# Splitting work on GpSimd and half of a broadcast copied on chip by ScalarE, in a recommendation tower (one core)

## The reference, cut to what matters

```python
e = jnp.stack([tbl_f[ids[:, f]] for f in range(39)], axis=1)      # (2048, 39, 16)
xk = x0 = e
for idx, (W, b) in enumerate([(w0, b0), (w1, b1), (w2, b2)]):     # W: (39, fk, 128), fk = 39, 64, 64
    z = relu(einsum('bhd,bkd,hks->bsd', x0, xk, W) + b[None, :, None])
    if idx != 2:
        xk = z[:, :64, :]; direct.append(z[:, 64:, :])
    else:
        direct.append(z)
logit = sum(concatenate(direct, axis=1), axis=-1)                 # (2048, 256)
h = relu(concat([logit, dense_ctx]) @ W_top1 + b_top1)
h = relu(h @ W_top2 + b_top2);  y = h @ W_top3
```

## Time and profile before

| | us |
|---|---|
| median of 3 runs | 2626.81 (2619.22 to 2628.51) |
| the profiled execution, its own time | 2621.27 |
| its span | 2619.4 |
| PE busy | 2487.5 (95%) |
| DVE busy | 2452.1 (94%) |
| POOL busy | 973.6 (37%) |
| ACT busy | 866.4 (33%) |
| mean share of 16 DMA engines | 0.8 to 0.9 in most of the span |

### The profile page before, as it was taken

How to read it: one execution, slowest core, us unless ns; L and a number is a source line. 1 busy time by engine, 2 the same in 40 slices (tenths; PEclk the granted TensorE clock), 3 DMA queues, 4 the chain that set the end, 5 groups by cost and what they waited for, 6 DMA issues and landing times.

```text
span 2619.4 us, 28223 instructions
## 1 busy us (share of the span) xinstructions
PE 2487.5 (95%) x7350; PEld 1370.7 (52%) x7350; DVE 2452.1 (94%) x2375; ACT 866.4 (33%) x853; POOL 973.6 (37%) x674
## 2 busy tenths in 40 slices
PE   0699999999999999999999999999999999999978
PEld 0355555555555555555555555555555555555546
DVE  2599999999999999999999999999999999999982
ACT  0133333233333323333332333333233333333325
POOL 7570542608163360726336071633607262000000
PEclk9899999999999999999999999999999999999999
DMA  3997888998888898888888988888898788888710
GB/s 82 224 213 176 193 176 194 193 201 193 182 189 179 191 194 196 197 181 192 179 192 188 205 195 181 187 178 190 188 204 214 163 188 177 191 181 195 176 46 8
DMA packets 184305, 469.76 MB, mean 179 GB/s; under 512 B 37746, under 2 KB 74211, under 8 KB 184275
## 3 DMA queue, kind: packets, MB, share of 16 engines
q1 hardware_dynamic: 160941, 461.79, 78.2%
q0 software_dynamic: 19968, 5.15, 2.1%
q10 hardware_dynamic: 3367, 2.48, 0.4%
HBM read 456.96 MB, written 12.33 MB: 179 GB/s over the span
## 4 chain that ended last, share of the span: by engine, by line
PE 38%; DVE 28%; DMA 15%; issue 13%; ACT 2%; SPq 1%; DVEq 1%; POOL 0%; ACTq 0%
PE zacc_a L811 17%; PE zacc_b L811 15%; DMA spread<-x_periods 14%; DVE prod L705 13%; DVE low L676 7%; DVE prod L693 5%; PE zacc_a L846 2%; PE zacc_b L846 2%; DVE high L676 1%; ACT maps L549 1%; DMA shifted<-x_periods 1%; ACT high L578 1%; ACT maps L548 1%; SPq L422 1%; DVE half L712 1%
## 5 line engine op out<-in xcount | busy, mean ns | idle before, releaser
L705 DVE TENSOR_TENSOR prod<-spread,maps 128x1024 f32<-128x1024 f32 (+1 forms) x1280 | 1493.8, 1208 | 27.8 <-DMA spread<-x_periods 18.0
L578 ACT ACTIVATE high<-prod 128x1024 fp32r<-128x1024 f32 (+2 forms) x544 | 575.0, 1057 | 1452.8 <-DVE prod L705 1207.0
L483 POOL DMA_INDIRECT landed<-in_tbl,rows_id x624 | 953.3, 1528 | 237.5 <-issue 235.5
L811 PE MATMUL zacc_a<-prod,w_plain 128*128 128x512 f32 (+2 forms) x1920 | 881.9, 595 | 19.7 <-DVE prod L693 15.0
L811 PE MATMUL zacc_b<-prod,w_plain 128*128 128x512 f32 (+2 forms) x1920 | 877.9, 593 | 5.3 <-DVE prod L705 5.3
L676 DVE TENSOR_TENSOR low<-prod,high 128x1024 fp32r<-128x1024 f32 (+1 forms) x480 | 581.7, 1212 | 0.0
L811 PEld LDWEIGHTS zacc_a<-prod,w_plain 128*128 128x128 f32 (+2 forms) x1920 | 363.8, 190 | 362.3 <-issue 328.1
L811 PEld LDWEIGHTS zacc_b<-prod,w_plain 128*128 128x128 f32 (+2 forms) x1920 | 363.9, 190 | 347.3 <-issue 308.4
L489 POOL TENSOR_TENSOR mark<-mark 128x1 f32<-128x1 f32 x30 | 16.6, 553 | 973.2 <-PE maps L858 967.6
L693 DVE TENSOR_TENSOR prod<-shifted,x_thrice 117x1024 f32<-117x1024 f32 (+1 forms) x224 | 264.8, 1214 | 50.8 <-DMA shifted<-x_periods 49.3
L846 PE MATMUL zacc_a<-low,w_high 128*128 128x512 f32 (+1 forms) x480 | 234.8, 570 | 12.2 <-DVE low L676 12.2
(11 more groups left out here) (101 smaller groups left out, 821.7 us busy)
## 6 DMA issues: line engine op xcount, KB each, us to landing
spread<-x_periods SPq DMA_DIRECT2D x608, 512.0 KB, 22.9
shifted<-x_periods SPq DMA_DIRECT2D x640, 156.0 KB
x_thrice<-x_periods SPq DMA_DIRECT2D x96, 156.0 KB
landed<-in_tbl,rows_id POOLq DMA_INDIRECT x624
x_periods<-x SPq DMA_DIRECT2D x32, 256.0 KB
spread<-x_periods SPq DMA_DIRECT2D x32, 256.0 KB, 26.3
features<-feat ACTq DMA_DIRECT2D x16, 128.0 KB, 5.4
spread<-features SPq DMA_DIRECT2D x4, 512.0 KB, 5.4
```

Of the source, the lines that this page charges most:

```text
L483: nc.gpsimd.indirect_dma_start(out=landed[:, f, :], out_offset=None, in_=tables[f], in_offset=bass.IndirectOffsetOnAxis(ap=rows_id[:, f:f ...
L578: nc.scalar.activation(high[0:rows, h, :], prod[0:rows, p, :], ACT.Copy).then_inc(s_round, 1)
L705: nc.vector.tensor_tensor(to, spread[0:rows, t, :], maps[0:rows, :], ALU.mult).then_inc(s_prod, 1)
L811: return nc.tensor.matmul(z[:, hf * BANK:(hf + 1) * BANK], w, x[:, hf * BANK:(hf + 1) * BANK], start=start, stop=stop)
```

## The change

Four things change together.

- The low part of 14 of the 47 tiles of a turn is made on GpSimd (new letter P); 10 tiles stay V and 23 are F (before 30 F, 17 V). No P stands in places 20 to 26. The ring of high parts has 4 buffers. The gathers no longer come in one go: they are put singly between GpSimd's low parts, two or more to each place in 20 to 26.
- `spread` is loaded for partitions 0 to 63 only, and the upper 64 are a copy of these by ScalarE (`double`, new, 20 in a turn: at places 41 to 46 and 0 to 13). VectorE's product waits for the copy.
- So that both halves can be equal, the maps stand in four blocks of 32 (maps 0 to 31 twice, then 32 to 63 twice), and a take of layer 0 or 1 writes four blocks and `direct01`: five instructions instead of three. The weights' rows are loaded in that order. The last tile has 128 rows now, with the last field twice, and its low part is made in place with signs.
- The channel sums on VectorE stand at other places (21 to 23 for layer 2, 26 to 28 for layer 1), next to the squares.

```diff
-PLAN = "FVFFVFFVFFVFFVFFFVFV" "FVFVFVF" "FVFFVFFVFFVFFVFFFVFV"
-NP, NH = 8, 3
+PLAN = "FPFVPFFPFPFVPFFPFPFV" "FVVFVVF" "FPFVPFFPFPFVPFFPFPFV"
+SPLIT = "VP"
+NP, NH = 8, 4
...
+DUP_AT = LAST[0] + 14
+SUM01_AT, SUM2_AT = N1 + LZ + 2, N1 + 1
...
-                    sp.dma_start(spread[h * HALF:(h + 1) * HALF, PIECE * q:PIECE * q + tiles, :],
-                                 src.unsqueeze(0).to_broadcast([HALF, tiles, COLS])).then_inc(s_spread[q], 16)
+                    sp.dma_start(spread[h * QUART:(h + 1) * QUART, PIECE * q:PIECE * (q + 1), :],
+                                 src.unsqueeze(0).to_broadcast([QUART, PIECE, COLS])).then_inc(s_spread[q], 16)
...
+            def low_part(turn, j):
+                rows, at_ = rows_of(j), slot(j, ALL, NP)
+                pool.wait_ge(s_round, n_kind(turn, j, SPLIT) + 1)
+                nc.gpsimd.tensor_tensor(low[0:rows, at_, :], prod[0:rows, at_, :], high[0:rows, slot(j, SPLIT, NH), :],
+                                        ALU.subtract).then_inc(s_lowp, 1)
...
-                nc.scalar.activation(to[0:HALF, :], z[0:HALF, :], ACT.Relu, bias=b[0:HALF, :])
-                nc.scalar.activation(to[HALF:128, :], z[0:HALF, :], ACT.Relu, bias=b[0:HALF, :])
+                for k, h in ((0, 0), (0, 1), (1, 0), (1, 1)):
+                    at_, part = k * HALF + h * QUART, slice(k * QUART, (k + 1) * QUART)
+                    nc.scalar.activation(to[at_:at_ + QUART, :], z[part, :], ACT.Relu, bias=b[part, :])
                 nc.scalar.activation(direct01[keep:keep + HALF, :], z[HALF:128, :], ACT.Relu,
                                      bias=b[HALF:128, :]).then_inc(s, 1)
+
+            def double(n, t):
+
+                if t % PIECE == 0:
+                    act.wait_ge(s_spread[t // PIECE], n.count(32, 32))
+                nc.scalar.activation(spread[HALF:128, t, :], spread[0:HALF, t, :], ACT.Copy).then_inc(s_double, 1)
...
-                    if t % PIECE == 0:
-                        dve.wait_ge(s_spread[t // PIECE], turn.count(32, 32))
+                    dve.wait_ge(s_double, turn.count(N1, t + 1))
```

More of the change, by code:

```diff
@@ L31 @@
 HALF = MAPS // 2
+QUART = HALF // 2
 ROWS = 128
@@ L108, in earlier, with gather_slots @@
                 return back, i
+def gather_slots():
+    free = [p for p in range(GATHER_AT + 1, 2 * TILES) if PLAN[p % TILES] != "P"]
+    among = [p for p in free if p % TILES in SQUARED]
+    rest = [p for p in free if p % TILES not in SQUARED]
+    need = FIELDS - len(among)
+    return sorted(among + [rest[i * len(rest) // need] for i in range(need)])
+GATHERS = gather_slots()
 class Turn:
@@ L273, in tail @@
         def tail(of):
-            split = [j for j in of if PLAN[j] == "V"]
+            split = [j for j in of if PLAN[j] in SPLIT]
             return split[-1] if split and split[-1] + LATE >= of[-1] else None
@@ L479, in _, with gather @@
             nc.gpsimd.memset(mark[:, :], 0.0).then_inc(s_mark, 1)
-            def gather():
-                for f in range(FIELDS):
+            def gather(first, last):
+                for f in range(first, last):
                     nc.gpsimd.indirect_dma_start(
@@ L567, in emit @@
                     act.wait_ge(s_const, 16 * 4)
-                if PLAN[j] == "V" and has(turn, j):
-                    h, p, rows = slot(j, "V", NH), slot(j, ALL, NP), rows_of(j)
+                if PLAN[j] in SPLIT and has(turn, j):
+                    h, p, rows = slot(j, SPLIT, NH), slot(j, ALL, NP), rows_of(j)
                     if j in SQUARED:
@@ L711, in channel_sum @@
                     dve.wait_ge(ready, turn.count(1, 1))
+                    if which == 1:
+                        dve.wait_ge(s_sum01, turn.count(1, 1))
+                    elif not turn.fixed or turn.number() > 0:
+                        dve.wait_ge(s_sum2, turn.count(1, 0))
                     nc.vector.tensor_tensor(half[:, :], src[:, 0:COLS // 2], src[:, COLS // 2:COLS], ALU.add
@@ L746, in emit @@
                     split_top()
-                if last.real() and 0 <= j - LZ - 2 < 3:
-                    channel_sum(last, 1, j - LZ - 2)
-                if last.real() and last.odd and j == LZ + 5:
+                sum2_at = LZ + 2 if turn.fixed and turn.number() == CHUNKS else SUM2_AT
+                if last.real() and 0 <= j - sum2_at < 3:
+                    channel_sum(last, 1, j - sum2_at)
+                if last.real() and last.odd and j == sum2_at + 3:
                     feature(last, 1)
@@ L870, in emit @@
                     then = step_back(turn, j, LATE)
-                    if then and PLAN[then[1]] == "V":
+                    if then and PLAN[then[1]] in SPLIT:
                         done = contract_low(*then)
```

117 lines of the change are left out of this document (75 added, 42 removed).

## The result

| | before | after |
|---|---|---|
| median, us | 2623.01 (2615.54 to 2628.51, 4 runs) | 2861.26 (2858.17 to 2866.3, 4 runs) |
| ratio | | 1.0912 (95% interval 1.0877 to 1.0948) |
| span of the profiled execution | 2619.4 | 2856.4 |
| mean granted clock | 0.992 | 0.951 |

The changed kernel is 9.1% slower; the prediction said 2840 (2700 to 2935). The pace comes first, as in the earlier trace rows: the takes of layer 2 of the kernel after, with ns min/median/max, first and last start.

What follows compares the result with a forecast made beforehand. TensorE and VectorE were both taken as full, TensorE alone after the change: 73.2 + 7.7 stalls + 1.5 clock + 0.6 GpSimd = 83.0 us a turn. With 205, 2 and 10 added to 2621.3: 2838, stated as 2840 (2700 to 2935).

Steps and rivals of the forecast that it cites:

- The turn's floor: TensorE's own work in a turn of the changed kernel, claimed as 73.2 us, with VectorE at 67.1 no longer a bound.
- First stall: TensorE at place 24, waiting for the rounding behind layer 1's longer take: 3.8 us a turn instead of 0.3.
- Second stall: TensorE at place 31, waiting for the rounding behind layer 0's take, itself behind product 30's rounding: 3.9 us, lower bound 2.8.
- The clock: TensorE running at its lower clock level after the stalls: 1.5 us a turn, bounds 0 and 6.0.
- GpSimd and VectorE: Delay where GpSimd's low parts meet VectorE instructions with two SBUF inputs: 0.6 us a turn, from 0 to 5.6.
- The rival in which both lock each other: VectorE also waits for GpSimd, 1.4 us for each of 14 low parts: 2946 us; chance 0.12.
- Doublings and DMA: ScalarE's 20 doublings a turn cost nothing, at most 1 us; halving the spread loads gains nothing.
- Start: Before the turns: longer takes, the first doubling and short VectorE preparations add 10 us.
- End: The last turn has no squares and takes the longer take once: 2 us more.
- Takes hidden: Rival: TensorE has enough work during takes, so a turn is 74.1 us, 2569 in all; chance 0.08.
- Only the first stall: Rival: second stall only 2.8 us and the clock never falls, a turn of 79.8, 2742 in all; chance 0.12.
- GpSimd the bound: Rival: GpSimd limits the turn if a low part takes 4.2 us or more; at 4.5, 2968 us; chance 0.04.

Runs made afterwards that it cites:

- e2: The changed kernel with layer 0 and 1 takes of three instructions instead of five (maps in wrong blocks, so other values are computed): 2780.12 us, ratio 1.0581.
- e8: The changed kernel with places 20 to 26 lettered FVFFFVF, giving plain tiles behind layer 1's release: 2850.73 us, ratio 1.0874.
- e1: The kernel before with takes of layers 0 and 1 in five instructions instead of three, nothing else: 2806.07 us, ratio 1.0675.
- e4: The changed kernel with low parts of places 15 and 17 moved to VectorE and 3 and 11 to GpSimd, in layers 1 and 2: 2845.85 us, ratio 1.0818.
- e3: The changed kernel without doublings, spread loaded whole by DMA: 2864.18 us, ratio 1.09.
- e9: The change's GpSimd part alone (whole loads, three-instruction takes), plus FVFFFVF at places 20 to 26 and layer 0's take split behind places 31 to 33: 2629.16 us.

## Why the prediction was right, and where its sizes were off

- **The turn's floor, 73.2.** Right as far as the terms below add up to the 83.35 - 73.2 = 10.2 that are left; DVE's 82% is as predicted.
- **First stall, 3.8.** 3.16 in the turn shown, 3.51 in the next. The take is 5.44 long as predicted (copies of 32 partitions 1.07 each, no shorter than one of 64).
- **Second stall, 3.9.** 4.19 in the turn shown, 3.0 in the mean, 2.64 in most. The predicted path, product 30 and its rounding ahead of the take, is the measured one in 13 of 31 turns. In the others the take starts as soon as PE has released it, which the prediction had as its lower bound of 2.8. And where the predicted path holds, it does so in 12 of 13 turns with a `feat` that GpSimd held up by 1.13 us; neither `feat` nor that hold was in my sum.
- **What I had not seen** is that the two are ends of one chain, 23.2 us against 15 of work in the turn shown. I had written the stalls down as the price of the takes, each by itself. That reading failed in e2 (110 us too low an expectation) and in e8 (its first theory 80 too low), and the effects do not add up: the longer takes cost 5.8 us a turn in the kernel before (e1), and taking them out of the changed kernel gives back 2.4 (e2).
- **The clock, 1.5.** Too small, the term that was mis-sized most: 3.4 a turn, and 2.7 in e1. I had argued that the first loss would be swallowed by the second stall. PE's waits for roundings are (111.1 + 98.7) / 31 = 6.8 a turn where I had 7.7; with 3.4 that is the whole 10.2 by which the turn lies above 73.2. So the turn came out near by luck in part: stalls of 0.9 and a term for GpSimd of 0.6 too much stood against 1.9 too little for the clock.
- **GpSimd and VectorE, 0.6.** The mechanism is there: VectorE loses 2.4 us of squares a turn (75 us in all). As a term of its own it has no place in the sum, which is full without it; it sits under the takes, in the second stall by way of `feat`, and in e4 it gave back 0.65 a turn, all of it clock. The rival in which both lock each other was right as a mechanism and priced far too high.
- **Doublings and DMA, nothing.** Right by e3. The stall of 1.06 us at 1045.94, in six turns, was not predicted; it stands behind layer 2's take, and I did not take it apart.
- **Start, 10.** 17.6. **End, 2.** 3.6. These 9.2 us and 30 x 0.35 for the turn are the 20 us by which the profiled execution (2858.2) lies above 2838.
- **The rivals.** Takes hidden: excluded by e1. Only the first stall: its stall of 2.8 is what most turns show, and it is the clock that excludes it, which fell behind 10 of 20 idle times of 2.5 to 3.0 us and behind 39 of 40 longer ones. GpSimd the bound: its low part is 2.39 in the median, and PE waited 4.5 us for it in the whole run. (By the terms given there, 4.5 us for a low part make 63 + 24 = 87.0 a turn and not 87.4.)

The Trainium skill's "SBUF — State Buffer" (Who interferes with whom) says that either engine, GpSimd or VectorE with two SBUF inputs, can lock the other out. The trace after agrees for the side that was open: the square of 4.85 us, and the `feat` of 1.41. The Trainium skill's "GPSIMD Engine Reference" (3.1) had led to an estimate of 2.25 us for the low part; 2.39 was measured.

## What to carry to other kernels

When work moves to another engine, add up the whole chain between two releases (take, first products, rounding, next take) and hold it against the work that the bound engine has in just that stretch; a sum over the turn, and single stalls, mislead, since a stall removed early comes back at the chain's end. Count two instructions more on an engine that is 33% busy at full price where others queue behind them, and add the clock, which cost half as much as the idle time here (3.4 us beside 6.8). Look at more than one turn: the stall shown first was not the usual one, and an instruction that lasts five times its usual length is waiting for something. Fill such a stretch with tiles that need nothing from the engines of the chain: with the take's instructions set apart, that was worth 124 us of 2754.

## What the runs showed of the hardware

- ScalarE's copy goes by columns: 16 x 1024 1013 ns, 32 x 1024 1071, 64 x 1024 1050 (SBUF to SBUF).
- GpSimd's subtraction of 128 x 1024 took 2336 ns at least, 2389 in the median and 3448 at most. VectorE's instructions with two SBUF inputs beside it waited for it to end: a square of 1.21 us lasted 4.85, a `feat` of 0.28 lasted 1.41.
- The idle time behind which the granted clock falls had no fixed bound here. Under 1.00 in the 4 us behind it: in the kernel after, none of 6 idle times of 1.0 us, 10 of 20 from 2.5 to 3.0, 39 of 40 from 3.1 on; in e1, 22 of 45 from 1.78 to 1.91 and all 15 of 2.2; in e9 none of 3 of 2.18. After it has fallen, the next plain tile takes 2.77 us instead of 1.88. In front of the change I had only 1.81 and 4.67; stalls of about 2 us were dearer than I took them for.
- VectorE's branch at the end of the loop took 0.25 to 0.30 us to the next instruction in the kernels without doublings and 2.7 to 9.2 in those with them; the cause is open.
